# Attention stage of a four-layer kernel: first maxima reduced over two banks at a time, middle parts of q and k cast on GpSimd

## The reference, cut to what matters

```python
def _L3_conv_ref(x, q_w, k_w, v_w):
    xf = x.reshape(b, din, hw)
    Q = jnp.einsum('kc,bcp->bkp', q_w, xf)
    K = jnp.einsum('kc,bcp->bkp', k_w, xf)
    V = jnp.einsum('vc,bcp->bvp', v_w, xf)
    S = jnp.einsum('bkp,bkq->bpq', Q, K)
    A = jax.nn.softmax(S, axis=-1)
    z = jnp.einsum('bpq,bvq->bvp', A, V)
...
x = x + _L3_conv_ref(_gn(x), L3_conv_q_w, L3_conv_k_w, L3_conv_v_w)
```

## Time and profile before

| | us |
|---|---|
| median of 3 runs | 1789.23 |
| lowest and highest | 1788.2, 1789.5 |
| the profiled execution, its own time | 1787.96 |
| its span in the trace | 1786.2 |
| mean granted clock of TensorE | 0.966 of full |

### The profile page before, as it was taken

How to read it: one execution, slowest core, us unless ns; L and a number is a source line. 1 busy time by engine, 2 the same in 40 slices (tenths; PEclk the granted TensorE clock), 3 DMA queues, 4 the chain that set the end, 5 groups by cost and what they waited for, 6 DMA issues and landing times.

```text
span 1786.2 us, 29864 instructions
## 1 busy us (share of the span) xinstructions
PE 1635.4 (92%) x10892; PEld 830.9 (47%) x10892; DVE 1239.0 (69%) x2443; ACT 1212.1 (68%) x2300; POOL 1102.3 (62%) x926
## 2 busy tenths in 40 slices
PE   5887899999988799999998979999999888999997
PEld 4464344444446344444443634444444454444442
DVE  5946777775684877777387388777748648777760
ACT  2045899988413689899732378999972337899994
POOL 2720478889751067888865016888887402788888
PEclk9988999999989999999998899999999899999998
DMA  2004000000000400000000040000000012000000
GB/s 88 1 1 90 1 6 7 7 7 6 11 1 1 90 2 6 7 7 12 6 6 1 3 88 1 6 11 7 7 6 6 0 26 29 2 11 7 7 7 11
DMA packets 12388, 26.83 MB, mean 15 GB/s; under 512 B 4560, under 2 KB 8912, under 8 KB 11728
## 3 DMA queue, kind: packets, MB, share of 16 engines
q1 hardware_dynamic: 12240, 24.92, 5.9%
HBM read 8.73 MB, written 6.42 MB: 8 GB/s over the span
## 4 chain that ended last, share of the span: by engine, by line
PE 67%; DVE 17%; ACT 8%; issue 5%; POOL 3%; POOLq 0%; DVEq 0%; ACTq 0%
PE PS L1315 25%; PE PS L1271 12%; PE PS L1241 11%; PE PS L1213 6%; DVE nmt L688 5%; PE PS L1169 3%; ACT Pb L956 3%; DVE nmt L681 3%; DVE Pb L595 3%; ACT PS L911 2%; PE PS L1128 2%; PE PS L1161 2%; PE PS L1204 1%; POOL accP L1076 1%; PE PS L1205 1%
## 5 line engine op out<-in xcount | busy, mean ns | idle before, releaser
L681 DVE TENSOR_REDUCE nmt<-PS 128x1 f32<-128x448 f32 x1176 | 681.2, 618 | 211.5 <-PE PS L1241 207.9
L1076 POOL TENSOR_TENSOR accP<-accP,Pb 128x512 f32<-128x512 f32 (+1 forms) x532 | 677.4, 1273 | 130.3 <-ACT Pb L956 82.2
L956 ACT ACTIVATE Pb<-PS 128x896 f32<-128x896 f32 (+1 forms) x700 | 636.5, 914 | 124.5 <-PE PS L1271 117.2
L1315 PE MATMUL PS<-Pb,VT 128*64 128x448 f32 x2800 | 660.9, 545 | 4.3 <-ACT Pb L956 3.6
L1241 PE MATMUL PS<-Ka,Qa 96*64 96x448 bf16 x2888 | 498.6, 356 | 23.5 <-ACT PS L911 10.7
L1271 PE MATMUL PS<-Qa,Ka 99*64 99x448 bf16 x2744 | 492.4, 354 | 3.0 <-ACT Pb L956 2.5
L911 ACT ACTIVATE PS<-PS,nmt 128x448 f32<-128x448 f32 x588 | 357.1, 607 | 33.6 <-DVE nmt L688 27.9
L1241 PEld LDWEIGHTS PS<-Ka,Qa 96*64 96x64 bf16 x2888 | 166.4, 110 | 269.6 <-issue 116.5
L1271 PEld LDWEIGHTS PS<-Qa,Ka 99*64 99x64 bf16 x2744 | 168.6, 110 | 242.1 <-issue 188.1
L1315 PEld LDWEIGHTS PS<-Pb,VT 128*64 128x64 f32 x2800 | 195.6, 137 | 104.1 <-ACT Pb L956 28.5
L834 ACT ACTIVATE xnp<-xw,nb,rstd 128x448 f32<-128x448 f32 x56 | 40.4, 749 | 195.3 <-DVE nb L503 195.3
(11 more groups left out here) (145 smaller groups left out, 1440.6 us busy)
## 6 DMA issues: line engine op xcount, KB each, us to landing
xin<-in_x SPq DMA_DIRECT2D x4, 1568.0 KB, 11.3
out<-xw SPq DMA_DIRECT2D x28, 224.0 KB, 1.9
Qa<-parts SPq DMA_DIRECT2D x24, 168.0 KB, 7.1
Ka<-parts SPq DMA_DIRECT2D x24, 112.0 KB, 4.0
Ka<-parts SPq DMA_DIRECT2D x24, 84.0 KB, 2.5
Qa<-mpt SPq DMA_DIRECT2D x96, 1.3 KB
wz<-in_weights SPq DMA_DIRECT2D x1, 829.0 KB, 7.7
Qa<-parts SPq DMA_DIRECT2D x24, 28.0 KB, 1.9
```

Of the source, the lines that this page charges most:

```text
L681: nc.vector.reduce_max(nmt[:, target % 2, b, t:t + 1], PS[0:BLK, bank, 0:CH], X, negate=True).then_inc(mx_free, 1)
L956: nc.scalar.activation(Pb[0:r, j % PSLOTS, :, :], PS[0:r, 2 * (k % 2):2 * (k % 2) + 2, 0:CH], ACT.Exp).then_inc(exp_done, 1)
L1076: nc.gpsimd.tensor_tensor((accQ if j < TO_ACCP else accP)[0:r, :, REST:CH], (accQ if j <= TO_ACCP else accP)[0:r, :, REST:CH], Pb[0:r, j % ...
L1315: last = mm(PS[C * h:C * h + C, OB, 0:CH], VT[:, j, C * h:C * h + C], Pb[:, j % PSLOTS, h, :], start=(j == 0), stop=(j == NQ - 1))
```

## The change

The 49 tiles are put together into 25 units: (b, t) with (b + 3, t) for b = 0, 1, 2 in each row t, after every odd t the pair (6, t-1), (6, t), and (6, 6) alone at the end. A unit takes two neighbouring banks, and there are three such slots, banks 0 to 5. PE writes both tiles of a unit and signals once; DVE reduces both banks in one instruction with two results for each partition; ACT sums the first tile of the unit where b < 3, as before. The columns of V are computed after the unit with b = 1, and ACT copies them after the sum of the unit with b = 2. After the last unit PE writes 3 times four tiles that nobody reads, where it was 7 times two. The middle parts are cast on POOL, all 7 behind its last work for the normalisation.

```diff
+    units = []
+    for t in range(NJ):
+        units += [((b, t), (b + ACT_BLOCKS, t)) for b in range(ACT_BLOCKS)]
+        if t % 2:
+            units.append(((NJ - 1, t - 1), (NJ - 1, t)))
+    return units + [((NJ - 1, NJ - 1),)]
...
+FIRST_SLOTS = 3
...
-                def first_tile(i):
-
-                    b, t = FIRST_ORDER[i]
-                    dve.wait_ge(first_ready, TILES * g + i + 1)
-                    nc.vector.reduce_max(nmt[:, 0, b, t:t + 1], PS[0:BLK, i % NJ, 0:CH], X,
+                def first_unit(u):
+
+                    slot, (b, t), (b2, t2) = 2 * (u % FIRST_SLOTS), FIRST_UNITS[u][0], FIRST_UNITS[u][-1]
+                    if b2 > b:
+                        peaks = nmt[:, 0, b:b2 + 1:ACT_BLOCKS, t]
+                    else:
+                        peaks = nmt[:, 0, b, t:t2 + 1]
+                    dve.wait_ge(first_ready, len(FIRST_UNITS) * g + u + 1)
+                    nc.vector.reduce_max(peaks, PS[0:BLK, slot:slot + len(FIRST_UNITS[u]), 0:CH], X,
                                          negate=True).then_inc(first_used, 1)
...
-                def middle_part(j):
-                    act.wait_ge(rest_h, NJ * g + j + 1)
-                    nc.scalar.activation(parts[:, 1, j * CH:(j + 1) * CH], rest[:, j, :],
-                                         ACT.Copy).then_inc(part_m, 1)
...
+                for u, unit in enumerate(FIRST_UNITS):
+                    b, t = unit[0]
                     if b < ACT_BLOCKS:
-                        act.wait_ge(first_used, TILES * g + i + 1)
-                        tile_sum(0, b, t, i % NJ).then_inc(first_summed, 1)
-                    if b == NJ - 1:
+                        act.wait_ge(first_used, len(FIRST_UNITS) * g + u + 1)
+                        tile_sum(0, b, t, 2 * (u % FIRST_SLOTS)).then_inc(first_summed, 1)
+                    if b == ACT_BLOCKS - 1:
                         value_part(t)
...
                 power(g, 3)
+                for j in range(NJ):
+                    pool.wait_ge(rest_h, NJ * g + j + 1)
+                    nc.gpsimd.tensor_copy(parts[:, 1, j * CH:(j + 1) * CH], rest[:, j, :]).then_inc(part_m, 1)
...
+                ready = [0] * FIRST_SLOTS + [sum(v[0][0] < ACT_BLOCKS for v in FIRST_UNITS[:u + 1]) for u in range(len(FIRST_UNITS))]
+                for u in range(len(FIRST_UNITS) + FIRST_SLOTS):
+                    slot = 2 * (u % FIRST_SLOTS)
+                    if u < FIRST_SLOTS:
+                        pe.wait_ge(rest_h, NJ * g + slot + 2)
                     else:
-                        pe.wait_ge(first_used, TILES * g + i - NJ + 1)
-                    if i >= TILES:
-                        for _ in range(2):
-                            tile_of(i % NJ, 0, NJ - 1, NJ - 1)
+                        pe.wait_ge(first_used, len(FIRST_UNITS) * g + u - FIRST_SLOTS + 1)
+                        if FIRST_UNITS[u - FIRST_SLOTS][0][0] < ACT_BLOCKS:
+                            pe.wait_ge(first_summed, ACT_TILES * g + ready[u])
+                    if u >= len(FIRST_UNITS):
+                        for _ in range(4):
+                            tile_of(slot, 0, NJ - 1, NJ - 1)
                         continue
...
+                    for n, (b, t) in enumerate(FIRST_UNITS[u]):
+                        if t == FIRST_KEYS and b == 0:
+                            pe.wait_ge(k_rest, 16 * (SPREADS * (g + 1) + 1))
+                        last = tile_of(slot + n, 0, b, t)
+                    last.then_inc(first_ready, 1)
+                    if FIRST_UNITS[u][0][0] == 1:
+                        value_columns(FIRST_UNITS[u][0][1])
```

More of the change, by code:

```diff
@@ L84, in order_first @@
 def order_first():
[L86 to L92, removed]
+    units = []
[4 more added lines that the diff above has]
+    return units + [((NJ - 1, NJ - 1),)]
+FIRST_UNITS = order_first()
+FIRST_SLOTS = 3
 def plan_banks():
@@ L798, in superblock @@
                             column_sums(sidx)
-                for i in range(TILES):
-                    first_tile(i)
-                dve.wait_ge(first_used, TILES * (g + 1))
+                for u in range(len(FIRST_UNITS)):
+                    first_unit(u)
+                dve.wait_ge(first_used, len(FIRST_UNITS) * (g + 1))
                 split_high(0)
@@ L892, in group @@
                     act.wait_ge(loaded, 16 * (SPREADS * g + 1))
-                for j in range(NJ + 2):
+                for j in range(NJ + 1):
                     if j < NJ:
                         normalise_chunk(rows(xnf[:, j * CH:(j + 1) * CH]), xw, j, xn_ready[3])
-                    if 1 <= j <= NJ:
+                    if j:
                         high_part(j - 1)
-                    if j >= 2:
-                        middle_part(j - 2)
                 def value_part(i):
@@ L1344, in group @@
                 pe.wait_ge(k_first, 16 * (SPREADS * (g + 1) + 1))
[L1345 to L1349, removed]
-                    else:
-                        pe.wait_ge(first_used, TILES * g + i - NJ + 1)
-                    if i >= TILES:
-                        for _ in range(2):
-                            tile_of(i % NJ, 0, NJ - 1, NJ - 1)
-                        continue
[L1356 to L1361, removed]
+                ready = [0] * FIRST_SLOTS + [sum(v[0][0] < ACT_BLOCKS for v in FIRST_UNITS[:u + 1]) for u in range(len(FIRST_UNITS))]
[3 more added lines that the diff above has]
+                        pe.wait_ge(rest_h, NJ * g + slot + 2)
+                    else:
+                        pe.wait_ge(first_used, len(FIRST_UNITS) * g + u - FIRST_SLOTS + 1)
[4 more added lines that the diff above has]
+                            tile_of(slot, 0, NJ - 1, NJ - 1)
+                        continue
+                    for n, (b, t) in enumerate(FIRST_UNITS[u]):
[5 more added lines that the diff above has]
+                        value_columns(FIRST_UNITS[u][0][1])
                 pe.wait_ge(v_ready, NJ * (g + 1))
```

## The result

| | before | after |
|---|---|---|
| median | 1789.4 us (4 runs) | 1818.5 us (4 runs, 1816.7 to 1820.6) |
| ratio to before, 95% interval | | 1.0164 [1.0152, 1.0177] |
| span of the profiled execution | 1786.2 us | 1818.8 us |
| mean granted clock | 0.966 | 0.947 |
| first tile to transposes, groups 0 to 3 | 28.7, 27.9, 28.3, 28.3 us | 34.7, 37.0, 37.2, 34.8 us |

The change costs 29 us, on the side that was forecast but twice the 14.7 us, and outside the range (1796 to 1812). The last row says where: of the 32.6 us that the spans differ by, 30.7 lie between PE's first tile of scores and its transposes in the four groups (143.8 us in all, 113.1 before). From the first product of q and k to the first tile it takes 12.0 us (12.4 in group 1) both before and after.

A forecast was written before the change was run, and what follows sets the result against it. DVE's reductions were taken to bound the first-maxima stage. Per group -1.5 + 3.4 + 0.9 - 0.4 = +2.4 us, 9.6 for four, plus 5.1 for the clock: 1789.2 + 14.7 = 1803.9 us, range 1796 to 1812.

The forecast's parts named there:

- What bounds the stage: First-maxima stage: DVE's back-to-back reductions are the bound, so every microsecond saved or lost there goes through to the end.
- The reductions: DVE's 49 reductions become 25, at 1.00 us per two-bank unit: 24.6 us against 26.11, -1.5 us for a group.
- The waits: DVE waits 1.04 us before unit (2, 5) in rows 1, 3 and 5, behind PE's V columns: +3.4 us a group.
- The end: Stage end: PE's longer unread tail starts the transposes 2.0 us after the last reduction, not 1.11: +0.9 us a group.
- the walk: Stepping through the lists of PE, DVE and ACT over all 25 units to place waits and the transposes' start.
- The start: Stage start: PE's first tile does not move, DVE's first reduction comes earlier if low parts are done: -0.4 us a group.
- the rival with slow casts: POOL casts cost as much as two inputs, DVE starts late, a group loses 6.0 us: 1813.2 us; chance 0.12.
- The clock: PE rests 3.2 us before the stage, clock falls to 1.2 GHz for 3.4 us: +1.7 us, three of four groups, 5.1.
- The other four terms: Reductions, waits, end and start of the stage together: +2.4 us for a group, +9.6 for four.
- The rival without a fall: PE's longer rest at the stage start brings no fall of the clock: 1789.2 + 9.6 = 1798.8 us; chance 0.22.
- the others: Remaining rivals: DVE stays the bound, 1785.2 us, chance 0.07; joining does little, a wash at 1789 to 1792, chance 0.07.

The follow-up runs named there:

- the run with all fills: Changed kernel plus matmuls nobody reads: 15 at each stage's start, five or six in rows 1 to 6; 1.0073, 1799.9 us against 1787.7 before.
- A shorter tail alone: Changed kernel with matmuls nobody reads at start and in rows, tail cut to 3 times two tiles; 1.0080 to before, 14.8 us over.
- the casts alone: Kernel before with only the middle-part casts moved to POOL, tiles still one by one; 1.0016 to before, 3.4 us slower in the medians.
- the start filled: Changed kernel with 15 matmuls nobody reads between the last product of q and k and the first unit; 1.0158 to before.
- V columns later: Changed kernel with the V columns computed after the unit with b = 2 instead of b = 1; 1.0062 to before, 11.2 us over.

## Why the prediction was right in its direction and wrong in its size

**What bounds the stage, and that losses there go through**: right. The stages account for 30.7 of the 32.6 us between the spans.

**The reductions** (-1.5 us for a group): too good. A unit takes 1.086 us and the next begins 1.03 after it ((7.28 - 1.09) / 6), in place of 1.00; without waits 25 take 25.2, so the gain is 0.9.

**The waits** (+3.4): right in place and nearly in size. The 1.04 us are 1.00, in rows 1, 3 and 5, when the clock holds, and there are no others: 3.0 for a group.

**The end** (+0.9): right at full clock. In the run with all fills, group 2, the last reduction ends at 1066.65 and the transposes start at 1068.65, the 2.0 of the walk. A shorter tail alone did not win it back: the stages got shorter, and the kernel did not get faster.

**The start** (-0.4, casts hidden): right for PE, whose first tile comes at the same distance as before. The casts were cheaper than feared: 0.55 us alone and 0.89 beside a low part, and the low parts, which I had made late by the common way into SBUF, keep their 0.61; it is POOL that waits. The last low part ends 0.1 to 0.7 us before PE's first tile. So the rival with slow casts was not it. The line of the Trainium skill on contention ("GPSIMD Engine Reference", Key points) agrees with these runs, with GpSimd as the one that pays, 0.34 us a cast, hidden here. The estimate of 0.6 us for one input, made by the same page's section Engine selection, is near the 0.55 of the undisturbed cast.

**The clock** (+5.1 in all): this is the step that failed. The fall at the start came, in four groups instead of three and for 7 us instead of 3.4, and its price was nearly right: +1.7 us was forecast for a group that has it, and it measured 1.73 with the casts alone and 2.0 with the units. But the sum had no term for the rows behind it. It reckoned the waits of 1.04 us only as time lost to DVE, and not as rests of PE, of which the new order makes more: in two rows 1.28, 0.46 and 1.03 us, where there were two of 0.98. Measured, the clock costs 17 us (changed kernel against all filled), 4.2 for a group, in place of 5.1 in all. By stages it is 20 us, of which 8 belong to the start and 12 to the falls in the rows and at the transposes, which the forecast put at nothing. The other four terms were +9.6; by the groups without a fall they are 10.5, since the slower unit adds 0.6 for a group and the shorter waits take 0.4 back.

The rival without a fall had 1798.8, near the 1799.9 of the run with the clock held by fills. That is in part luck, since two falls at the end still stand in that run, and for this kernel the rival was wrong. None of the others came.

## What to carry to other kernels

When an edit adds a wait behind which TensorE stands, add up the rests that it gives TensorE over the whole stretch, before and after. If they grow, the work on both sides of them may run at half the clock, and that can cost more than the wait: here 17 us at least, against 10 to 12 for the order itself. Try a few matmuls that nobody reads in the longest rest before giving up an edit that seemed hidden: with 15 of them at the start, the half of this change that alone cost 0.16% gains 0.28%. And when work for several consumers is joined in larger units, look first at what comes between two units in the producer's list: moving the V columns by one unit was worth 18 us, joining the reductions 0.95 us a group at best, and nothing in the stage as a whole.

## What was not expected of the hardware

- The clock's falls were not tied to one long rest. With rests of 1.28, 0.46 and 1.03 us in about 5 us it fell; with rests of 0.98 in every 3.72 it held in three groups of four; with rests of 0.42 to 0.46 before most units (V columns later) it held for 20 us in group 3, and with rests of 0.54, 0.43 and 0.43 (the same order, casts on ACT, short tail) it fell 5 to 6 us after the first tile of group 0. Which rests bring a fall is open.
- A fall that is prevented in one place came in another: with the start filled, three of four groups had a fall 5 to 6 us after their first tile, one of them for nearly 14 us.
- DVE with two inputs in SBUF and POOL with one: DVE kept 0.61 us, POOL went from 0.55 to 0.89. With POOL adding two inputs it was DVE that stood still. Why it is the one or the other is open; beside a cast of 0.89 us, the low part was always the first to start, by 0.13 to 0.14 us.
- The reduction over 896 elements takes 1.086 us and over 448 in the same kernel 0.615: 1.05 ns for each further element, where 49 to 448 elements gave 1.01.
